# One block for convolution and attention, expert weights loaded in place, and layer norm folded into the projection

## What is computed

```
xs = einsum('bhwc,dc->bhwd', x, W1) + b1          # 192 -> 48
xs = gelu(xs); xs = fft_low(xs)                   # low pass over 16 x 16, absolute value
x  = x + einsum('bhwd,cd->bhwc', xs, W2) + b2
t  = tokens(x)
t  = t + attn(ln(t), Wq, bq, Wk, bk, Wv, bv)      # 12 query heads, one key and value head, rotary
t  = t + ffn(ln(t), gate_w, gate_bank, up_bank, down_bank)   # softmax, top 2 of 8, silu(a) * u
```

## Time and profile before

| | |
|---|---|
| median of 3 runs | 443.9 us (442.26 to 444.21) |
| the profiled execution | 445.19 us, span 443.4 us, mean granted clock of TensorE 0.864 |
| PE, PEld busy | 357.6, 342.0 us |
| DVE, ACT, POOL busy | 276.6, 217.4, 276.1 us |
| HBM read, written | 25.75, 14.98 MB |

### The profile page before, as it was taken

One profiled execution on the slowest core, in us unless ns is written; L12 is line 12 of the kernel. 1 busy time (PEld: TensorE's weight loads), 2 busy tenths in 40 slices (PEclk: granted clock), 3 DMA queues, 4 the chain that ended last, 5 costly groups with the idle time before them and its releaser, 6 DMA issues.

```text
span 443.4 us, 8897 instructions
## 1 busy us (share of the span) xinstructions
PE 357.6 (81%) x2163; PEld 342.0 (77%) x2164; DVE 276.6 (62%) x747; ACT 217.4 (49%) x518; POOL 276.1 (62%) x301
## 2 busy tenths in 40 slices
PE   4686724776867461598999999999999999999990
PEld 4686724665766451487999999999999999999990
DVE  2276786489766567992656565656565656566650
ACT  2464632414643430682555555555555555555550
POOL 0255775486786502004578888888888888888763
PEclk9786876995998555556999999999999999999996
DMA  6979791002243253002244444444444444444442
GB/s 193 268 213 269 172 276 53 0 2 83 83 131 120 84 167 77 0 0 63 46 74 77 71 77 69 80 66 79 67 77 69 75 74 72 75 72 77 74 49 27
DMA packets 45814, 41.03 MB, mean 93 GB/s; under 512 B 14041, under 2 KB 39868, under 8 KB 45788
## 3 DMA queue, kind: packets, MB, share of 16 engines
q0 software_dynamic: 13824, 16.98, 23.5%
q1 hardware_dynamic: 31964, 23.77, 19.5%
HBM read 25.75 MB, written 14.98 MB: 92 GB/s over the span
## 4 chain that ended last, share of the span: by engine, by line
PE 51%; DMA 1%; POOLq 0%; issue 0%; POOL 0%; ACT 0%; DVE 0%; SPq 0%; ACTq 0%; DVEq 0%
PE moe_ps_y L1198 9%; PE moe_ps_h L1184 5%; PE moe_ps_gt L1173 3%; PE moe_ps_u L1173 3%; PE moe_ps_gt L1177 3%; PE moe_ps_gt L1174 3%; PE moe_ps_gt L1176 3%; PE moe_ps_u L1174 3%; PE moe_ps_gt L1175 3%; PE moe_ps_y L1200 3%; PE moe_ps_u L1177 3%; PE moe_ps_u L1175 3%; PE moe_ps_u L1176 3%; PE moe_ps_x L1164 2%; PE moe_ps_x L1165 2%; PE moe_ps_y L1197 2%
## 5 line engine op out<-in xcount | busy, mean ns | idle before, releaser
L1137 POOL DMA_INDIRECT out<-moe_y,idx_map x71 | 113.0, 1591 | 29.3 <-issue 20.1
L1129 POOL DMA_INDIRECT moe_xt<-rows,idx_map x71 | 69.8, 984 | 57.2 <-POOLq L958 30.8
L1281 ACT ACTIVATE moe_yy<-moe_ps_y,moe_xt 128x384 f32<-128x384 f32 x71 | 41.3, 582 | 71.1 <-PE moe_ps_y L1198 71.1
L1198 PE MATMUL moe_ps_y<-wd,moe_h_hi 128*128 x213 | 70.1, 353 | 0.6 <-DVE moe_h_lo L1344 0.6
L1352 DVE TENSOR_TENSOR moe_y<-moe_yy 128x192 f32<-128x192 f32 x71 | 25.5, 360 | 56.5 <-ACT moe_yy L1281 56.5
L1261 ACT ACTIVATE moe_x_hi<-moe_ps_x 128x256 fp32r<-128x256 f32 x71 | 27.4, 386 | 33.8 <-PE moe_ps_x L1165 33.7
L1344 DVE TENSOR_TENSOR moe_h_lo<-moe_ps_h,moe_h_hi 128x384 fp32r<-128x384 f32 x71 | 39.6, 558 | 2.7 <-ACT moe_h_hi L1273 0.5
L1198 PEld LDWEIGHTS moe_ps_y<-wd,moe_h_hi 128*128 128x128 f32 x213 | 40.2, 189 | 1.2 <-issue 1.2
L1328 DVE TENSOR_TENSOR moe_x_lo<-moe_ps_x,moe_x_hi 128x128 fp32r<-128x128 f32 x71 | 20.7, 292 | 30.8 <-ACT moe_x_hi L1261 30.8
L1338 DVE TENSOR_TENSOR moe_hid<-moe_ps_u,moe_sg 128x384 f32<-128x384 f32 x71 | 38.9, 548 | 0.0
L1200 PE MATMUL moe_ps_y<-wd,moe_h_lo 128*128 x142 | 35.6, 251 | 0.0
(11 more groups left out here) (214 smaller groups left out, 1023.1 us busy)
## 6 DMA issues: line engine op xcount, KB each, us to landing
xs<-in_x SPq DMA_DIRECT2D x8, 384.0 KB, 6.3
conv_stage<-in_wgu SPq DMA_DIRECT2D x8, 384.0 KB, 4.2
conv_stage<-in_wgu SPq DMA_DIRECT2D x16, 192.0 KB, 4.9
rows<-attn_xr SPq DMA_DIRECT2D x8, 384.0 KB, 2.7
out<-xs SPq DMA_DIRECT2D x8, 384.0 KB, 3.2
wd<-in_down SPq DMA_DIRECT2D x8, 288.0 KB, 4.4
conv_xta<-in_xT SPq DMA_DIRECT2D x8, 256.0 KB, 4.6
moe_xt<-rows,idx_map POOLq DMA_INDIRECT x71, 2.8
```

The lines of the kernel that those rows point to most:

```text
L1129: nc.gpsimd.indirect_dma_start(xt[:, slot, :], None, rows.ap(), bass.IndirectOffsetOnAxis(ap=idx_map[:, j, 0:1], axis=0)).then_inc(gathere ...
L1137: nc.gpsimd.indirect_dma_start(out, bass.IndirectOffsetOnAxis(ap=idx_map[:, j, 1:2], axis=0), y[:, j % YR, :], None, compute_op=ALU.add).t ...
L1198: ins = nc.tensor.matmul(both, hi, halves, start=(k == 0), stop=(k == 2))
L1281: nc.scalar.activation(yy[:, s].rearrange("p h c -> p (h c)"), ps_y[:, s, 0:2 * C], ACT.Copy, scale=xt[:, slot, bass.ds(GC + e, 1)]).then_ ...
```

## The change

`conv_phase` and `attention_phase` become one block, `front_phase`, all of it written out without loops of the chip. There is no barrier between them: PE turns and projects quad 0 around its last `out_product`, in the same PSUM banks (`ps_a`, `ps_b` are `ps_w1`, `ps_q` is `ps_c`, `ps_ra`, `ps_rb` are `ps_f`).

All transposed images have room of their own, so image and row loads wait for nothing. `stage` is gone: an expert's weights land in `w_lo`, where the low part will stand (one DMA of 6 KB a partition each), ACT copies the high parts from there and the subtraction is done in place. The images lie in the memory of `wa_hi` and `wb_hi`, the small convolution tiles in that of `wd`; so `split(e)` on ACT also waits for `w1_done` of quad e, and `wd` is loaded after the last `out_product`. `x` comes in laid out by partition, with two columns of padding per tile.

The norm ahead of the projection is not applied to the tile. `xs` has two more columns, C and C + 1: mean and variance from `bn_aggr`, the latter turned by POOL's `in_deviation` into the standard deviation. They are transposed with the tile and meet two rows of `wqb`: the negative column sums of the weights (made once by `column_sums`) and the bias. What PE makes then lacks only the factor `rstd` of each token: `copy_key_value` (four ACT instructions with a scale for two without) and `scores` (four `scalar_tensor_tensor` of 192 for two `tensor_tensor` of 384) multiply by it. `norm` on DVE and its buffer are gone, and so are PE's `keep_busy` products of the attention block.

The splits are dealt anew: in the convolution ACT makes the high parts of the first experts and POOL `wa_lo` of experts 0 to 4, one quad after another; DVE does all `wb_lo`, `wa_lo` of experts 5 to 7, and `wd` of experts 0 to 4, in the attention loop; POOL does `wd` of experts 5 to 7 at the end. `copy_key_value(n + 1)` now stands right behind `exponential(n)`, and the early exponential ahead of `norm_route`. In `expert_phase` only addresses change: `wd` is stored half by half, so the 384 columns are two runs of 192.

```diff
+DOWN_AT = {2: (0,), 3: (1, 2), 4: (3, 4), 5: (5, 6), 6: (7,)}
...
+            place("room_a", [P, EXPERTS * 6 * C - used + EXPERTS * 2 * HID - TOKENS])
+            early.append(place("xta", [P, TOKENS]))
+            place("room_b", [P, EXPERTS * 2 * HID - TOKENS])
+            early.append(place("xtb", [CB + 1, TOKENS]))
+        wd = keep("wd", [P, EXPERTS, 2, 3 * C], F32R)
         wa_hi = keep("wa_hi", [P, EXPERTS, 2 * HID], F32R)
-        wa_lo = keep("wa_lo", [P, EXPERTS, 2 * HID], F32R)
         wb_hi = keep("wb_hi", [P, EXPERTS, 2 * HID], F32R)
...
+        ps_a, ps_b = ps_w1[:, 0], ps_w1[0:CB + 2, 1]
+        ps_ra, ps_rb = ps_f[:, 0], ps_f[:, 1]
+        ps_q = ps_c
...
+                def load_rows(q):
+                    sp.dma_start(xs[:, bass.ts(q, QT), :].rearrange("p t c -> p (t c)"),
+                                 x[:, bass.ts(q, QT * XC)]).then_inc(x_in[q], 16)
+                def load_weights(e):
+                    sp.dma_start(w_lo[:, e].rearrange("p b h -> p (b h)").bitcast(F32), wgu[:, e, :]).then_inc(w_in[e], 16)
...
+                for q in range(3, QUADS):
+                    load_turned(q)
+                    load_rows(q - 1)
+                    if q > 3:
+                        load_weights(q - 4)
+                load_rows(last)
+                sp.dma_start(eye[:], ident).then_inc(tables_in, 16)
+                for dst, src in tables:
+                    sp.dma_start(dst, src).then_inc(tables_in, 16)
+                for e in range(4, EXPERTS):
+                    load_weights(e)
+                sp.dma_start(desc[:], desc_table).then_inc(desc_in, 16)
+                sp.wait_ge(filled, 3)
+                sp.dma_start(rows[TOKENS:TOKENS + P, :], zero[:]).then_inc(stored, 16)
+                sp.wait_ge(w2_done, made(last))
+                for e in range(EXPERTS):
+                    sp.dma_start(wd[:, e, 1, :].bitcast(F32), down[:, e, :]).then_inc(down_in, 16)
...
+                def column_sums():
+                    pe.wait_ge(wq_in, 3 * 16)
+                    pe.wait_ge(filled, 2)
+                    nc.tensor.matmul(ps_f[0:CB + 1, 1, 0:QW], sel[:], wqa[:], start=True, stop=False)
+                    nc.tensor.matmul(ps_f[0:CB + 1, 1, 0:QW], sel[0:CB, :], wqb[0:CB, :], start=False,
+                                     stop=True).then_inc(sum_done, 1)
...
+                def turn(q):
+                    pe.wait_ge(in_dev, made(q))
                     pe.wait_ge(ev_done, q + RING)
-                    transposes(nc, xn[:, s], eye, ps_a, ps_b).then_inc(tr_done, 1)
-                def project(i, s):
-                    q = quad(i, s)
+                    for t in range(QT):
+                        nc.tensor.transpose(ps_a[:, bass.ts(t, P)], xs[:, QT * q + t, 0:P], eye[:])
+                        ins = nc.tensor.transpose(ps_b[:, bass.ts(t, P)], xs[:, QT * q + t, P:XC], eye[:])
+                    ins.then_inc(tr_done, 1)
+                def project(q):
...
+                pe.wait_ge(bias_row, 2)
+                in_product(2)
+                column_sums()
+                pe.wait_ge(sum_out, 1)
+                lowpass_product(1)
...
+                    out_product(q - 2)
+                lowpass_product(last)
+                out_product(last - 1)
+                pe.wait_ge(tables_in, 16 * (len(tables) + 1))
+                pe.wait_ge(gelu_done, made(last))
+                turn(0)
+                out_product(last)
+                pe.wait_ge(added, made(last - 1))
+                project(0)
+                turn(1)
+                pe.wait_ge(added, made(last))
                 for n in range(QUADS + LAG_OUT):
-                        project(*turned(0, n))
                     if n + 1 < QUADS:
-                        turn(*turned(0, n + 1))
+                        project(n + 1)
...
+                copy_key_value(0)
+                out_of_psum(1)
                 for n in range(QUADS + LAG_OUT):
                     if n < QUADS:
-                        copy_key_value(*turned(0, n))
+                        exponential(n)
                     if n + 1 < QUADS:
-                        out_of_psum(*turned(0, n + 1))
+                        copy_key_value(n + 1)
+                    if n + 2 < QUADS:
+                        out_of_psum(n + 2)
                     if n >= LAG_OUT:
-                        copy_logits(*turned(0, n - LAG_OUT))
+                        copy_logits(n - LAG_OUT)
                     if 0 <= n - LAG < QUADS:
-                        route_out_of_psum(*turned(0, n - LAG))
-                    if n < QUADS:
-                        exponential(*turned(0, n))
-                    if 0 <= n - RING < QUADS:
-                        norm_route(*turned(0, n - RING))
-                    if n < 4:
-                        split(4 + n)
+                        route_out_of_psum(n - LAG)
                     if n == EARLY // QT + LAG_OUT - 1:
                         act.wait_ge(early_less, 1)
                         nc.scalar.activation(pr[:, 0:EARLY], lg[:, 0:EARLY], ACT.Exp).then_inc(early_ex, 1)
+                    if 0 <= n - RING < QUADS:
+                        norm_route(n - RING)
+                    if n < EXPERTS - 5:
+                        split(5 + n)
+                    if n == 2:
+                        act.wait_ge(down_in, 16 * EXPERTS)
+                    for e in DOWN_AT.get(n, ()):
+                        split_down(e)
...
+                    nc.gpsimd.tensor_tensor(rstd[:, at], vtmp[:, s, :], half[:, 0:1].broadcast_to([P, QT]),
+                                            ALU.pow).then_inc(in_pow, 1)
+                    pool.wait_ge(in_pow, made(q))
+                    pool.sem_inc(pool_turn, 1)
+                    nc.gpsimd.tensor_tensor(xs[:, at, C + 1], vtmp[:, s, :], rstd[:, at], ALU.mult).then_inc(in_dev, 1)
...
+                    nc.gpsimd.tensor_tensor(shift[:, at], minus[:, s, :], rstd[:, at], ALU.mult).then_inc(dev_done, 1)
+                for q in range(QUADS - 1):
+                    in_deviation(q)
+                    if q > 1:
+                        split(q - 2)
+                pool.wait_ge(tables_in, 16 * (len(tables) + 1))
+                rotate_key(0)
+                in_deviation(last)
                 for n in range(QUADS):
                     if n + 1 < QUADS:
-                        rotate_key(*turned(0, n + 1))
-                    weigh_value(*turned(0, n))
+                        rotate_key(n + 1)
+                    weigh_value(n)
                     if n:
-                        deviation(*turned(0, n - 1))
-                    if n < EXPERTS - 3:
-                        split(3 + n)
-                deviation(last, 1)
+                        deviation(n - 1)
+                deviation(last)
+                for e in range(5, EXPERTS):
+                    split_down(e)
...
-                            prod[:, t], both[:, :, 0:C].rearrange("p t (h d) -> p t h d", h=HEADS),
-                            bcast(kk[:, s, t, :], 2, HEADS), ALU.mult)
+                    for t in range(QT):
+                        ins = nc.vector.scalar_tensor_tensor(
+                            out=prod[:, t], in0=ps_q[:, s, t // 2, (t % 2) * QW:(t % 2) * QW + C].rearrange("p (h d) -> p h d", h=HEADS),
+                            scalar=rstd[:, bass.ds(QT * q + t, 1)], in1=bcast(kk[:, s, t, :], 1, HEADS), op0=ALU.mult, op1=ALU.mult)
...
+                split(0)
+                for n in range(QUADS):
+                    scores(n)
                     if n:
-                        residual(0, n - 1)
-                    weights(0, n)
-                with dve.Fori(1, last) as i:
-                    for s in range(RING):
-                        norm(i + 1, s)
-                        scores(i, s)
-                        residual(i - 1 + s, 1 - s)
-                        weights(i, s)
-                for s in range(RING):
-                    scores(last, s)
-                    residual(last - 1 + s, 1 - s)
-                    weights(last, s)
-                residual(last, 1)
+                        residual(n - 1)
+                    weights(n)
+                    if n + 1 < EXPERTS:
+                        split(n + 1)
+                    if 2 < n:
+                        split_down(n - 3)
+                residual(last)
...
-                        halves = wd[:, bass.ds(e, 1), k].rearrange("p e h c -> p (e h c)")
-                        high = wd[:, bass.ds(e, 1), k, 0].rearrange("p e c -> p (e c)")
+                        halves = wd[:, bass.ds(e, 1), :, bass.ts(k, C)].rearrange("p e h c -> p (e h) c")
+                        high = wd[:, bass.ds(e, 1), 0, bass.ts(k, C)].rearrange("p e c -> p (e c)")
```

782 lines of the change are left out of this document (325 added, 457 removed).

## The result

| | before | after |
|---|---|---|
| median | 443.64 us (442.26 to 444.21, 4 runs) | 418.12 us (417.07 to 420.31, 4 runs) |
| profiled execution | 445.19 us, span 443.4 | 418.42 us, span 416.5 |

The account below looks back on a forecast made before the run. TensorE bounds the expert stage; chains or order bound convolution and attention, where VectorE becomes the bound after the change. The block ends at 143.7 instead of 166.4, 22.7 us less: 445.2 becomes 422.5, median 421 us, range 408 to 436.

Parts of the forecast that it names:

- Convolution: Convolution stage: without the wb_lo split 4.3 us a quad, 1 us for late weights; last aggregate at 51.8, not 66.37.
- Seam: Between convolution and attention: block end and pipeline fill vanish, POOL's queue sets the first score product at 56.3 us.
- Loop: Attention quads, bound by VectorE: 6.9 us, 7.3 twice, 8.8, 31.4 for quads 4 to 6, then 6.5; weights(7) ends at 124.5.
- the pointer product: Attention's score product as four VectorE instructions with a scalar by pointer: 1.6 us a quad instead of 1.05.
- the holds: VectorE's splits and POOL's pv delay each other: 0.84 us in quad 3, 1.68 in quads 4 to 6, 5.9 together.
- End and tail: Behind weights(7): 0.7, 1.8 and 2.8 us to T at 129.8; then 13.9 us to the block's end at 143.7.
- T: Time at which residual(7), the attention loop's last, has its last aggregate: forecast 129.8 us, 152.07 before.
- The rule on SBUF: Attention loop: the skill page's exclusion would hold residual some 0.8 us in eight quads, 6 us more; the sum held nothing.
- Rival B: Merged attention loop: TensorE at 1.2 GHz needs 12.2 us a quad in the last five, +14 us, 435 us; chance 0.24.
- A: Attention loop: the holds cost little and products run at the old rate, 5.9 + 4.4 us less, 411 us; chance 0.18.
- C: Front: a late load or queue order keeps the first score near 75 us, T near 149, 441 or more; chance 0.04.
- D: Expert stage: down product reads two runs at half rate, 0.16 us more a product, +35 us, 456 us; chance 0.03.

Follow-up runs that it names:

- e6: Changed kernel with TensorE turning quad 0 only after the convolution's last finish has added, so no overlap at the seam: 424.1 us.
- e1: Changed kernel with VectorE's splits from quad 3 on placed between scores and residual instead of behind weights: 412.8 us.
- e2: Changed kernel without VectorE's wa_lo splits of experts 5 to 7 and wd splits of experts 0 to 4: 408.8 us.
- e4: Changed kernel with ScalarE's key and value copy, and what follows it, put back behind norm_route and the splits: 432.3 us.
- e5: Changed kernel with unread products added on TensorE where it idles in the attention loop and its tail: 416.3 us.
- e8: Changed kernel with loads of expert weights 1 to 3, and those behind, held until the previous expert's high parts are made: 425.2 us.
- e7: Changed kernel with wb_lo of experts 0 to 2 moved back into the convolution loop: 418.15 us.
- e3: Changed kernel with four unused VectorE operations of the old norm's kind and size added in seven quads: 427.3 us.

## Why the prediction was right, step by step

**The sum.** It gave 422.5 us for a profiled execution, and 418.4 was measured. The 4.1 us are spread over small terms, most on the side of too long, and some of the closeness is luck, as misses of both signs meet in it.

- Convolution, 1.4 us: the quads took 4.05 to 4.45 us where I had 4.3, and ScalarE did not wait for expert 3's weights (its split began at 38.51 right behind other work), for which I had added 1 us. The 296 GB/s of the first 52 us are above the estimate of 255. One slip: 23 + 5 x 4.3 is 44.5 and not 44.3, so my own terms end at 52.0 and the sum at 422.7.
- Seam, 0.4 us: 4.12 against 4.5. POOL's queue did set it. The exclusion is there, but on the other side than I had it: VectorE's wb_lo took 1.95 us at 50.29, POOL's split its usual 1.80, and POOL then lost 0.7 us in its first rotation instruction. That the fill vanishes was right, and e6 prices it at 6.0 us.
- Loop, 1.6 us, from errors that partly cancel. Quads 4 to 6 took 29.5 us and not 31.4: the pointer product took 1.42 us to the next instruction where I had taken 1.6 (8 x 0.18 over the loop), and the holds, put at 1.68 us as two halves of pv, are 1.52 - 0.87 for wa_lo and 1.31 - 0.67 for wd (the free values are steps of e1), 1.3 a quad. On the other side quad 1 took 8.42 us instead of 7.3, by the lower clock, which the sum had left out. Quad 3 agrees (8.60, 8.8) for another reason than I gave: 0.2 us of hold instead of 0.84, and 0.68 us of waiting for kk.
- End and tail, 0.6 us: 4.98 against 5.3 behind weights(7), and 13.56 against 13.9 from T to the gates. The 13.9 were meant for the router steps of quads 6 and 7, which end last by my account; they do, at 140.19, 14.1 us behind T.

**What bounds the loop.** VectorE, as the prediction said, in quads 4 to 6 without waiting for another engine; e2 shows it from the other side, since what is taken from VectorE there comes off T. In quads 0 to 3 VectorE still waited for kk (2.23, 1.42 and 0.68 us), and the prediction had only the first of these. That the round over POOL and ScalarE was opened is shown by e4, which closes it again and pays 14 us.

**The rule on SBUF.** After the change residual began at 88.00, inside POOL's pow, and took its usual time, as in the earlier trace rows; VectorE, then POOL:

```profile
88.00 0.95 DVE L721 TENSOR_TENSOR xs<-xs,front_pv 128x768 f32<-128x768 f32 x1
```

```profile
87.54 1.04 POOL L606 TENSOR_TENSOR rstd<-front_vtmp,front_half 128x4 f32<-128x4 f32 x1
```

The rule of the Trainium skill's page SBUF — State Buffer (section "SBUF: two separate sides"), which is for a GpSimd instruction that reads SBUF, as pow does, and not for any, as I had put it, would have held one of the two for the whole of the other. Here neither was held, and the sum was right to leave this out. For large operands the trace agrees with the rule: pv 2.87, wa_lo 1.59, wd 1.39 us together, 1.63, 0.95 and 0.75 apart. A short operation that begins inside a long one is held as well: 0.62 us for vtmp.

**Rival B.** The lower clock came as the rival said. Projection 2 ran at 1.2 GHz behind a wait of 3.26 us for ScalarE:

```profile
59.24 1.14 PE L346 MATMUL front_ps_c<-wqa,front_xa 128*128 128x240 f32 x2 [3.26 <-ACT front_xb L450]
```

and the score product behind it was late, by 1.42 us:

```profile
69.85 1.39 DVE L695 SCALAR_TENSOR_TENSOR front_prod<-front_ps_c,rstd,front_kk 128x192 f32<-128x192 f32 x4 [1.42 <-POOL front_kk L582]
```

Its price was off by far: B had 14 us, e5 finds 1.8 by the medians and some 2.5 in the timelines. The step of B that fails is its count of 12.2 us in each of five quads: only projections 2, 4 and 7 ran at the lower level, 1, 3, 5 and 6 at the upper, and projection 7 was covered by a quad of 9.86 us in which VectorE never waited. In the tail every router step is at the lower level, 5.55 us from one transposition to the next:

```profile
129.18 1.51 PE L358 MATMUL front_ps_f<-eye,front_xr 128*128 128x128 f32 x6 [0.33 <-issue]
...
134.73 1.51 PE L358 MATMUL front_ps_f<-eye,front_xr 128*128 128x128 f32 x6 [0.33 <-issue]
```

and these steps end the block, but the choice on VectorE ends only half a microsecond before; in e5, where they are fast, the tail is 0.8 us shorter. The Trainium skill's page TensorE: Matmul & The Clock Gate (section on oscillation) has TensorE fall to the lower level again and again where its products are shorter than its waits. The trace agrees in part, in three of the eight projections; it costs little because most of what it slows is covered.

**Rivals A, C and D.** A's time of 411 is nearly e1's, reached by moving the splits: where the change has them, the holds do cost, some 4 us of e1's 5.3. Its other half, the product at the old rate, did not come (1.42 against 1.05). C is refuted at the first score product. D is refuted by the down product's row: two runs of 192 cost 0 ns more than one of 384.

**What the prediction did not say.** It read the old convolution as quads back to back of 5.08 us. In the trace before only the one from 28.96 took that; from 34.04 on they took 7.98, 6.22 and 5.54 us. Over the convolution TensorE waited 3.86, 1.59, 3.46 and 2.41 us for images, and VectorE behind it. TensorE, then VectorE, in the kernel before:

```profile
37.17 0.79 PE L249 MATMUL conv_ps_w<-conv_w1a,conv_xta 128*128 128x128 f32 x2 [3.46 <-DMA conv_xtb<-in_xT]
```

```profile
42.02 0.42 DVE L411 TENSOR_TENSOR conv_g_lo<-conv_g,conv_g_hi 128x256 fp32r<-128x256 f32 x1 [2.04 <-ACT conv_g_hi L311]
...
48.24 0.42 DVE L411 TENSOR_TENSOR conv_g_lo<-conv_g,conv_g_hi 128x256 fp32r<-128x256 f32 x1
```

The forecast of the convolution's end did not suffer, as it was counted up from absolute times with the loads free. But it named the split as what makes a quad shorter and gave the loads no price, and of the 16.0 us the loads are the larger part: e8 gives 8.8 back by holding them, while seven splits of 0.84 us are an estimated 5.9. Neither was tried in the kernel before. e7 shows that the place of three of the splits is worth nothing in the end.

And the fold takes 1.6 us a quad of norms off VectorE and adds 0.37 in the product. The splits that moved in are more than that: the loop of the kernel after is 3.2 us longer than the one before. In this kernel the norms would cost 6.5 us at T (e3), so the fold pays for much of the move.

## What to carry to other kernels

Where VectorE and GpSimd both work on SBUF, place a long operation by what the other engine does at that moment, not only by who has time: the same three subtractions cost 1.3 us less a quad before the residual than behind the weights. When an engine has work in front of a hand-over, look for the round that it closes, and move the hand-over ahead of what nobody waits for. In a stage fed by DMA, look over all its tiles for waits on loads before one tile is taken as its period, and let the loads run ahead.

## What the runs showed of the hardware

- A POOL pow over 128 x 4 elements, 1.04 us by itself, let a VectorE addition of 128 x 768 with both inputs in SBUF run beside it unhindered when that began 0.46 us after it (88.00 and 87.54), and took 1.86 us when a VectorE subtraction began 0.02 us after it (86.03 and 86.01, e1). Which part of it excludes VectorE was not tried.
- The level of TensorE's clock at a given instruction differs between executions of the same instructions: projection 0 took 0.57 us a pair in the change's profile and 1.01 in e5's, whose program for TensorE does not differ up to there, and the first score product came 1.4 us later. In the change's, TensorE had worked from 40.21 on almost without a gap and had been at the lower level from 41.09 to 44.40; in e5's it had been at the upper level until 42.91 and idled 1.73 us before 44.65.
- A moving operand of 384 columns in two runs of 192 cost what one run of 384 did: 353 ns, the mean over 213 products, before and after.
